# A second level of the product sum on VectorE, and the attention output's variance ahead of the first norm

## What is computed

```python
# part 1: a long convolution of outer products, gated into x
kv = einsum('bhil,bhjl->bijhl', k_, v_)            # k_ = v_ = the context, 32 heads of head_dim 8
y = irfft(rfft(kv) * rfft(ssm_kernel))[..., :L]     # causal convolution along L = 512
out = y + kv * D
out = einsum('bijhl,bhil->bjhl', out, q_)           # q_ = layernorm(x); a sum over i of 8 products
x = x + tanh(g_xattn) * out
# part 2: linear attention with a routed feature map, gated into x
x = silu(x_prev * conv_w[:, 0] + x * conv_w[:, 1])  # on layernorm(x)
q = silu(x @ Wq); k = x @ Wk; v = x @ Wv; g = x @ Wg
q, k = rotary(q), rotary(k)                         # then scaled by a softmax / one-hot of v @ router_w
qk = einsum(q_exp, k_exp) * HDK ** -0.5 * tril
o = einsum('bhlm,bhmd->bhld', qk, v)
o = (o - mean(o)) / sqrt(var(o) + 1e-5)             # per head of 32 values
x = x + tanh(g_ffn) * ((silu(g) * o) @ Wout)
```

## Time and profile before

| | us |
|---|---|
| median of 3 runs | 931.52 (929.35 to 932.26) |
| the profiled execution's own time | 932.18 |
| its span, first to last instruction | 930.1 |
| PE busy | 867.2 (93%) |
| DVE busy | 708.1 (76%) |
| POOL busy | 699.6 (75%) |
| ACT busy | 420.0 (45%) |

### The profile page before, as it was taken

One profiled execution on the slowest core, in us unless ns is written; L12 is line 12 of the kernel. 1 busy time (PEld: TensorE's weight loads), 2 busy tenths in 40 slices (PEclk: granted clock), 3 DMA queues, 4 the chain that ended last, 5 costly groups with the idle time before them and its releaser, 6 DMA issues.

```text
span 930.1 us, 18000 instructions
## 1 busy us (share of the span) xinstructions
PE 867.2 (93%) x6656; PEld 734.9 (79%) x6656; DVE 708.1 (76%) x1496; ACT 420.0 (45%) x906; POOL 699.6 (75%) x613
## 2 busy tenths in 40 slices
PE   0678999999999999999999999999999999999973
PEld 0467888888888888888888888888888888888762
DVE  4867878788778787877778788778787887777642
ACT  2454454444454544444444444544544444544220
POOL 6578788777777987777788877777987777786331
PEclk9889999999999999999999999999999999999995
DMA  8211220122222201222221122222101222210000
GB/s 280 61 52 52 63 56 20 51 63 63 64 63 64 47 22 58 63 64 63 64 63 34 32 61 64 63 63 63 51 20 56 63 64 63 63 46 13 3 11 21
DMA packets 25989, 52.44 MB, mean 56 GB/s; under 512 B 2544, under 2 KB 3696, under 8 KB 25904
## 3 DMA queue, kind: packets, MB, share of 16 engines
q1 hardware_dynamic: 22304, 46.59, 18.5%
q10 hardware_dynamic: 3600, 4.72, 1.6%
HBM read 42.75 MB, written 8.55 MB: 55 GB/s over the span
## 4 chain that ended last, share of the span: by engine, by line
PE 83%; issue 5%; DVE 4%; DMA 3%; POOL 2%; ACT 1%; POOLq 0%; ACTq 0%; SPq 0%; DVEq 0%
PE bank L314 36%; PE bank L288 22%; PE bank L266 9%; PE bank L275 6%; PE bank L300 4%; PE bank L347 3%; PE bank L332 3%; DMA x_in<-in_x 2%; DMA w_all<-in_L_ffn_Wv 1%; POOL o_rstd L638 1%; DVE z_terms L745 1%; DVE w_all L708 0%; POOL rstd L638 0%; PE bank L397 0%; POOLq L66 0%
## 5 line engine op out<-in xcount | busy, mean ns | idle before, releaser
L288 PE MATMUL bank<-kv_high,toep 128*128 128x512 f32 x640 | 224.8, 409 | 11.0 <-DVE z_terms L736 5.7
L632 POOL TENSOR_TENSOR kv_low<-kv,kv_high 128x576 fp32r<-128x576 f32 x128 | 182.3, 1436 | 49.5 <-ACT kv_high L482 49.5
L623 POOL TENSOR_TENSOR kv<-kx 128x512 f32<-128x512 f32 x128 | 173.9, 1358 | 6.6 <-DMA const<-shape_consts 6.6
L288 PEld LDWEIGHTS bank<-kv_high,toep 128*128 128x128 f32 x640 | 122.4, 191 | 42.2 <-DVE z_terms L736 12.2
L638 POOL TENSOR_TENSOR o_rstd<-o_ve,minus_half 128x16 f32<-128x16 f32 x32 | 93.1, 2908 | 76.4 <-DVE o_ve L814 76.4
L482 ACT ACTIVATE kv_high<-kv 128x576 fp32r<-128x576 f32 x128 | 87.8, 688 | 114.1 <-POOL kv L626 114.1
L288 PE MATMUL bank<-kv_low,toep 128*128 128x512 f32 x320 | 126.9, 396 | 0.0
L314 PE MATMUL bank<-w_all_high,yT_high 128*128 128x512 f32 (+2 forms) x512 | 119.9, 356 | 2.6 <-DVE gated L841 2.5
L745 DVE TENSOR_TENSOR z_terms<-z_terms 128x512 f32<-128x512 f32 (+1 forms) x96 | 116.7, 1242 | 0.1
L314 PE MATMUL bank<-w_all_low,yT_high 128*128 128x512 f32 (+2 forms) x512 | 112.5, 341 | 0.0
L314 PE MATMUL bank<-w_all_high,yT_low 128*128 128x512 f32 (+2 forms) x512 | 106.5, 340 | 0.0
(11 more groups left out here) (102 smaller groups left out, 1673.3 us busy)
## 6 DMA issues: line engine op xcount, KB each, us to landing
toep<-taps_dram SPq DMA_DIRECT2D x32, 512.0 KB, 7.1
kx<-in_ctx SPq DMA_DIRECT2D x32, 384.0 KB, 7.4
x_in<-in_x SPq DMA_DIRECT2D x32, 256.0 KB
out_x<-out_sb SPq DMA_DIRECT2D x32, 256.0 KB
w_all<-in_L_ffn_Wv ACTq DMA_DIRECT2D x1, 1024.0 KB, 12.6
w_all<-in_L_ffn_Wg ACTq DMA_DIRECT2D x1, 1024.0 KB, 11.1
w_out<-in_L_ffn_Wout ACTq DMA_DIRECT2D x1, 1024.0 KB, 17.2
router<-in_L_ffn_router_w ACTq DMA_DIRECT2D x1, 512.0 KB, 7.1
```

The source lines that it names most:

```text
L288: ins = nc.tensor.matmul(bank[lc % 2][:, :], toep[:, 1 - p, a, (lc - mc) * P:(lc - mc + 1) * P], kv_p[b][:, 1 - p, mc, 0:FULL], start=(mc ...
L623: eng.tensor_tensor(view(kv[:, c % 2, 0:FULL], [[ROW, NROT], [1, ROW]]), view(kx[:, p, c, 0:ROW], [[0, NROT], [1, ROW]]), view(kx[:, p, c, ...
L632: eng.tensor_tensor(kv_p[1][:, p, c, :], kv[:, c % 2, :], kv_p[0][:, p, c, :].bitcast(F32), ALU.subtract).then_inc(kv_ready[c], 1)
```

## The change

Three things are changed. `add_halves` is followed by a second instruction, `add_quarters`, that adds the upper two remaining terms onto the lower two; it waits for the first through a new semaphore `half_done`. Chunks 2 and 3 are now done together. PE then has two transposes per chunk, 8 a step, and its wait for chunk 2 is now for the sum of chunks 2 and 3. On DVE the two instructions that give `o_ve` stand ahead of the first norm's statistics, and on POOL the 16-column power stands ahead of the 1-column one.

```diff
-                    eng.wait_ge(sum_done[max(c, 1)], h1 + 1)
-                    for i in range(NROT):
+                    eng.wait_ge(sum_done[c | 1], h1 + 1)
+                    for i in range(NROT // 2):
...
+                if tail:
+                    rsqrt(o_rstd, o_ve, RH, o_ve_ready, h, o_rstd_ready)
                 if pre:
                     rsqrt(rstd1, ve1, 1, ve1_ready, h + 3, rstd1_ready)
-                if tail:
-                    rsqrt(o_rstd, o_ve, RH, o_ve_ready, h, o_rstd_ready)
...
-                                  ALU.add).then_inc(sum_done[chunks.stop - 1], 1)
+                                  ALU.add).then_inc(half_done[chunks.stop - 1], 1)
+            def add_quarters(chunks, h1):
+                eng.wait_ge(half_done[chunks.stop - 1], h1 + 1)
+                quarter = NROT * ROW // 2
+                eng.tensor_tensor(z_terms[:, chunks, 0:quarter], z_terms[:, chunks, 0:quarter],
+                                  z_terms[:, chunks, quarter:2 * quarter], ALU.add).then_inc(sum_done[chunks.stop - 1], 1)
...
                     add_halves(slice(0, 2), h + 1)
+                    add_quarters(slice(0, 2), h + 1)
...
                     multiply(p, 3, h + 1)
-                    add_halves(slice(2, 3), h + 1)
-                    add_halves(slice(3, 4), h + 1)
+                    add_halves(slice(2, 4), h + 1)
+                    add_quarters(slice(2, 4), h + 1)
```

More of the change, by code:

```diff
@@ L194, in flamingo_gated_layer @@
         y_low, gatedT_ready = sem("y_low"), sem("gatedT_ready")
+        half_done = [sem(f"half_done{i}") for i in range(CH)]
         sum_done = [sem(f"sum_done{i}") for i in range(CH)]
@@ L272, in add_transposed @@
                 for c in range(CH):
-                    eng.wait_ge(sum_done[max(c, 1)], h1 + 1)
-                    for i in range(NROT):
+                    eng.wait_ge(sum_done[c | 1], h1 + 1)
+                    for i in range(NROT // 2):
                         ins = nc.tensor.matmul(bank[2][:, c * P:(c + 1) * P], z_terms[:, c, i * ROW:(i + 1) * ROW], ident,
-                                               is_transpose=True, start=(c == 0 and i == 0), stop=(i == NROT - 1),
+                                               is_transpose=True, start=(c == 0 and i == 0), stop=(i == NROT // 2 - 1),
                                                skip_group_check=True)
@@ L793, in step @@
                                       ).then_inc(y_low, 1)
+                if tail:
+                    eng.wait_ge(o_squared, h)
+                    eng.tensor_reduce(o_var[:, :], o_sq[:, :, :], AX_X, ALU.add).then_inc(o_summed, 1)
+                    eng.wait_ge(o_summed, h)
+                    eng.wait_ge(eps_ready, h)
+                    eng.scalar_tensor_tensor(out=o_ve[:, :], in0=o_var[:, :], scalar=1.0 / HDV, in1=eps_w[:, :],
+                                             op0=ALU.mult, op1=ALU.add).then_inc(o_ve_ready, 1)
                 if pre:
@@ L807, in step @@
                     multiply(p, 2, h + 1)
[L808 to L815, removed]
                 if front:
```

## The result

The changed kernel takes 996.19 us (median of 4 runs, 995.3 to 996.46), against 931.44 for the kernel before: ratio 1.0696, with a 95% interval of 1.0682 to 1.0709. It is 7% slower. The profiled execution's span is 994.0 us against 930.1.

The account below looks back on a forecast made before the run. PE bounds the kernel. Per full step 2.8 us of waiting less 0.84 saved gives +2.0; 29 steps make 58, with the edges 61, on 932.2: 993 us, own range 982 to 1,004, wider range 960 to 1,006.

Parts of the forecast that it names:

- PE has no spare time, the last sum has 0.05: PE, 93% busy, sets the time; DVE's last sum is finished 0.05 us before PE's fourth chunk wants it.
- DVE and POOL take turns by whole instructions: DVE instructions with two SBUF inputs and POOL instructions reading SBUF exclude each other; whichever starts first runs to its end.
- half-rate reading: DVE and POOL share the port at half rate instead: 1,019 us; chance 0.04 together with D.
- The first pair of sums: DVE's sums of chunks 0 and 1 meet POOL's rotary work: double sum about 2.3 us, `gated` ends at 468.8.
- The second pair: DVE's sums of chunks 2 and 3: double sum behind L664, quarter sum behind L623, last sum ends at 473.35.
- V 1.95 and then 0.8: On PE the V projection starts 1.95 us later, then PE waits 0.8 for the last sum.
- The edges: First two steps (h = -1 and 0) lose about 1.2 us each, h = 30 about 0.2.
- the clock as a rival: D: PE's waits lower its clock in 3 of 29 full steps, 1,068 us; chance 0.04 together with half-rate reading.
- POOL's power hinders nobody.: POOL's power doesn't hold up DVE's sums: the double sum at 464.55 lies inside it.
- Rival A: Turns don't add up, each new DVE sum costs just itself: +1.0 us a step, 964 us; chance 0.20.
- B: Chunks 2 and 3 meet no lock on DVE, so faster: 0.7 us a step gained, 912 us; chance 0.09.

Follow-up runs that it names:

- e4: e3 without any quarter sum, 16 transposes a step: double sum of chunks 0 and 1 ahead of sel, one double sum for chunks 2 and 3; 931.55 us.
- e3: Kernel before with double and quarter sum of chunks 0 and 1 ahead of sel, one double sum for chunks 2 and 3, 12 transposes; 918.24 us.
- e2: Changed kernel with the moved variance and power lines put back, so only the second-level sums and 8 transposes; 965.24 us.
- e5: Changed kernel with POOL's rotary and product instructions made short, same number and order, outputs not the layer's; 926.85 us.
- e6: Kernel before with the same shortening of POOL's rotary and product instructions, outputs not the layer's; 928.59 us.
- e7: Changed kernel without the quarter sum of chunks 2 and 3, keeping the move, 12 transposes a step; 987.25 us.
- e8: e3 with the move of the variance and the power put back in; 925.0 us.
- e12: e3 with DVE's one-time output_weights_low instruction in step h = 0 moved behind the second norm's statistics; 916.55 us.

## Why the prediction was right, and where its steps were not

*PE has no spare time, the last sum has 0.05.* Right in the main. e4 shows that PE sets the time: a shorter DVE path gives nothing. e3 shows that PE's transposes are worth their length if DVE's sums stay in time. That the last sum has hardly any slack is seen in e2, where it ended 1.0 later and PE waited 1.34; the 0.05 itself is a reading of rows that no run tests.

*DVE and POOL take turns by whole instructions.* Right, and shown by e5 and e6: the same DVE work with short POOL instructions makes 926.85 instead of 996.19, while before gains 2 to 3 us from them. The half-rate reading is out by the time (1,019) and by the rows: in e2 and e3 the sum that comes 0.08 or 0.09 first takes 1.23, its length alone, and only POOL's instruction is longer, by 1.0. Two that shared the port would both be.

*The first pair of sums.* Right in each number: first double sum 2.34, `gated` at 467.93 for 468.15, V at 468.66 for 468.8.

*The second pair.* The end is right (473.48 for 473.35), the way is not. I had the double sum take its turn behind L664 and the quarter sum wait for L623. It lost the first turn by 0.16 us, waited for L623 itself (2.15), and the quarter sum then had only the short L626 ahead of it (0.69). The wait changed its owner, not its length. That the end came out right in spite of it is in part luck: e7, forecast by the same reckoning, has no quarter sum behind the lost turn and missed by 14 us.

*V 1.95 and then 0.8.* V's start is 1.83 later than before on the step's clock. The third chunk's transposes would have followed at 506.35 + 0.42 = 506.77 and start at 507.90, 1.13 later. The recorded idle times, 1.59 and 0.96, are shorter by some 0.2 each, as they count from the end of the instruction before, and the next one otherwise starts ahead of that end. 1.83 + 1.13 less the 0.84 saved is 2.1; PE is through at 473.95 on the old clock for 473.8. A whole step is 2.06 longer for 2.0: 29 × 2.06 = 59.6 against 58. So V was put 0.12 too late and the third chunk's wait 0.33 too short, and the two partly offset each other.

*The edges.* Mis-sized: the first two steps lost 5.2 for the 2.4 I gave them, and h = 30 and the end gained 0.9 where I had a loss of 0.2. Of the 5.2, 2.5 is the clock; the other 2.7 are near the forecast. I had named the clock as a rival for the full steps, where it kept to 1.00 at 91% busy; it fell in h = 0, behind the wait of 3.38 us. From the scores of h = 29 to those of h = 30 the changed kernel takes 27.60 for 27.30, close to the 0.2; what gains is the next stretch (22.09 for 23.64), where V waits 0.20 for 1.45. e2 and e3 gain there as well, e5 does not, and I have no cause for it. The sum of the edges, 4.3 for 2.6, is half of what the forecast of 993 lacks; the rest is 1.6 in the full steps.

*"POOL's power hinders nobody."* True of the sums inside it. But e8 shows that it takes a turn at its own start and can be held up: 1.51 us for 0.55.

Rival A (turns don't add up, 964) is what e2 alone gives, where the order of the powers is the old one: its last sum ends 1.0 later, and waits for one POOL instruction (1.64), as in before (1.76). No run reached B's 912; the nearest is e3, which puts the first pair of sums elsewhere and takes only four transposes off PE.

## What to carry to other kernels

Where VectorE and GpSimd both work from SBUF, as here, the price of one more two-input VectorE instruction can be its own length plus one whole GpSimd instruction. So look for a place where GpSimd runs something that doesn't hold the sum up, here its power, and put the sum there: e3's quarter sum cost nothing. Before filling or advancing an engine that seems idle, see what it will run into: here the earlier POOL start cost 0.63 us a step with no work added. Which of two instructions waits can hang on 0.1 us, so state a forecast for the end of the chain rather than for a link of it, and ask what the end would be with the turn lost: where nothing stood behind the turn (e7) the end moved too.

## What the runs showed of the hardware

- Where VectorE's two-input sum from SBUF and a GpSimd instruction that reads SBUF meet, the one that comes first runs at its own length and the other waits for all of it: by 0.08 us ahead the sum took 1.23 and GpSimd's L666 2.28 (e3); 0.04 us behind, the sum took 2.34 (changed kernel).
- GpSimd's `pow` on one column waits for a running two-input VectorE instruction: 1.51 us for 0.55 (e8), 2.52 for 0.55 (e12). Once running, the 16-column one (2.91) lets a double sum through at 1.22.
- During a single wait of 3.38 us TensorE's granted clock fell to 0.50 (1.2 GHz), and was back at 1.00 some 5.5 us after work had begun again; with repeated waits of 1.59 and 0.96 in each 28.8 us step it was 1.00 over 760 us.
